# Cross-attention with float32 probabilities: score products in bursts of three pairs, softmax sums inverted as 128x16 by way of DRAM, last iteration's divide and split placed in the next stage's block

## The reference

```
q = (layernorm(x) @ Wq + bq)   k = (ctx @ Wk + bk)   v = (ctx @ Wv + bv)      # x 4096x512, ctx 3202x512
A = softmax(q k^T / sqrt(32))                     # per head, 4096 x 3202
x = x + (A v) @ Wo + bo
y = layernorm(x);  w = softmax(y @ WrT + br), all but the two largest set to 0
x = x + sum_e w[e] * (y @ We[e]^T + be[e])
```

## Time and profile before

| | |
|---|---|
| time, median of 3 runs | 2689.87 us (2685.3 to 2693.89) |
| the profiled execution, time | 2697.49 us |
| its span, first to last instruction | 2695.7 us |
| attention block, first score product to the next block's first load | 302.3 to 2212.3 us |
| TensorE busy over the span | 2560.7 us (95%) |
| VectorE busy | 2298.3 us (85%) |
| ScalarE busy | 1910.6 us (71%) |
| GpSimd busy | 383.2 us (14%) |
| mean granted TensorE clock | 0.97 of 2.4 GHz |

### The profile page before, as it was taken

One profiled execution on the slowest core, in us unless ns is written; L12 is line 12 of the kernel. 1 busy time (PEld: TensorE's weight loads), 2 busy tenths in 40 slices (PEclk: granted clock), 3 DMA queues, 4 the chain that ended last, 5 costly groups with the idle time before them and its releaser, 6 DMA issues. The chain is left out here.

```text
span 2695.7 us, 42991 instructions
## 1 busy us (share of the span) xinstructions
PE 2560.7 (95%) x14123; PEld 1286.6 (48%) x14123; DVE 2298.3 (85%) x1810; ACT 1910.6 (71%) x2141; POOL 383.2 (14%) x324
## 2 busy tenths in 40 slices
PE   8999399999999999999999999999999969879998
PEld 7878233333333333333333333333333327768776
DVE  4377399999999999999999999999999966657555
ACT  3123388888888888888888888888888845523333
POOL 2122100000000000000000000000000014315664
PEclk9999699999999999999999999999999989969999
DMA  7446841000051100005110000511000028724463
GB/s 254 160 153 213 189 120 39 22 21 20 21 118 24 37 20 21 21 21 118 25 36 21 20 21 20 118 28 33 21 21 21 21 67 310 250 83 132 126 216 125
DMA packets 125744, 222.77 MB, mean 83 GB/s; under 512 B 19666, under 2 KB 51930, under 8 KB 124772
## 3 DMA queue, kind: packets, MB, share of 16 engines
q1 hardware_dynamic: 110468, 177.57, 23.3%
q0 software_dynamic: 15072, 42.49, 5.0%
HBM read 146.67 MB, written 91.14 MB: 88 GB/s over the span
## 5 line engine op out<-in xcount | busy, mean ns | idle before, releaser
L964 ACT ACTIVATE probs<-psum 128x1024 f32<-128x1024 f32 x1664 | 1612.1, 1024 | 244.4 <-PE psum L1088 215.2
L1017 DVE TENSOR_TENSOR sums<-sums,probs 128x2048 f32<-128x2048 f32 x704 | 1647.3, 2340 | 44.8 <-ACT probs L964 19.4
L1088 PE MATMUL psum<-q_st,k_st 97*128 97x512 f32 x3328 | 1004.8, 423 | 49.5 <-DMA q_st<-shift_scratch 23.6
L1088 PEld LDWEIGHTS psum<-q_st,k_st 97*128 97x128 f32 x3328 | 563.0, 189 | 825.4 <-ACT probs L964 673.7
L1095 PE MATMUL psum<-probs,v_st 128*32 128x512 f32 x6656 | 890.1, 607 | 0.0
L821 POOL TENSOR_TENSOR o_low<-o_sb,o_high 128x512 fp32r<-128x512 f32 x32 | 74.4, 2325 | 1791.3 <-ACT o_high L938 1791.3
L1095 PEld LDWEIGHTS psum<-probs,v_st 128*32 128x32 f32 x6656 | 131.5, 108 | 308.2 <-ACT probs L964 219.1
L1764 PE MATMUL psum<-we_hi,wo 128*128 x624 | 219.7, 414 | 8.5 <-issue 5.8
L1617 ACT ACTIVATE wo<-psum 128x512 fp32r<-128x512 f32 x78 | 46.8, 600 | 138.3 <-PE psum L1750 101.8
L1764 PEld LDWEIGHTS psum<-we_hi,wo 128*128 128x128 f32 x624 | 120.4, 193 | 35.3 <-issue 9.6
L1674 DVE TENSOR_TENSOR res<-psum,be_all 128x512 f32<-128x512 f32 x78 | 53.9, 691 | 93.3 <-PE psum L1764 92.3
(11 more groups left out here) (184 smaller groups left out, 1890.6 us busy)
## 6 DMA issues: line engine op xcount, KB each, us to landing
q_st<-qh_scratch SPq DMA_DIRECT2D x64, 256.0 KB
token_rows<-rows SPq DMA_DIRECT2D x8, 1040.0 KB, 5.2
xn<-in_x SPq DMA_DIRECT2D x16, 512.0 KB, 6.6
qh_scratch<-o_hi SPq DMA_DIRECT2D x8, 1024.0 KB, 4.5
ql_scratch<-o_lo SPq DMA_DIRECT2D x8, 1024.0 KB, 7.7
q_st<-ql_scratch SPq DMA_DIRECT2D x32, 256.0 KB
token_rows<-in_x SPq DMA_DIRECT2D x1, 8192.0 KB, 30.4
oh_scratch<-o_high SPq DMA_DIRECT2D x128, 64.0 KB, 1.6
```

The costliest lines, as they stand in the source:

```text
L964: nc.scalar.activation(probs[:, p_slot[t], 2 * half:2 * half + 2, :], psum[:, 2 * slot:2 * slot + 2, :], ACT.Exp, scale=SCALE).then_inc(ex ...
L1017: nc.vector.tensor_tensor(sums[b][:], a[:], probs[:, p_slot[t]], ALU.add).then_inc(added, 1)
L1088: mm = nc.tensor.matmul(psum[:, 2 * slot + h % 2, :], k_st[:, h, t * P:(t + 1) * P], q_st[:, b, h, :], start=True, stop=True)
```

## The change

Five things:

- **Bursts.** TensorE's pairs are no longer issued two per tile: before a weigh, pairs are issued up to an index that closes a set of three slots. `weigh(t)` follows pair 2t+7 or up to two more (`LEAD` = 7), so bursts of three pairs alternate with one and with two weighs.
- **Sums inverted small.** ScalarE copies the sums out of PSUM before pair 14 (128x512). GpSimd writes their 4 distinct rows to DRAM and reads them back as 128x16. VectorE inverts those after its 10th add, GpSimd writes the inverses to DRAM and reads them back with four DMAs, each spreading one row over 32 partitions. VectorE multiplies after its 14th add (before: both after the 5th).
- **Split later.** ScalarE's `o_high` moves from before pair 24 to before pair 36.
- **Last iteration.** Its sum copy, inversion, product, split and stores move into `route_tokens`, among its first five steps.
- **Buffers.** `recip`, `o_sb`, `o_high`, `o_low` become one shared tensor, which `route_tokens` uses for `yn` and `mix_experts` for `xs` and one `res`; some semaphores are merged (`fold`, `chain`).

```diff
-DIVIDE_AT = 4
+SUMS_COPY_AT, INVERT_AT, NORMALISE_AT, SPLIT_AT = 14, 9, 13, 36
+LEAD = 7
...
+def spread_sums(pool, a, it):
+    pool.wait_ge(a["sums_copied"], it + 1)
+    pool.dma_start(a["sum_d"], a["recip"][0:P:DH, :]).then_inc(a["bounced"], 16)
+    pool.wait_ge(a["bounced"], it * 32 + 16)
+    pool.dma_start(a["spread"][:], a["sum_d"].rearrange("h (p f) -> (h p) f", p=DH)).then_inc(a["sums_spread"], 16)
+def broadcast_inverses(pool, a, it):
+    pool.wait_ge(a["inverted"], it + 1)
+    pool.dma_start(a["inv_d"].rearrange("h (p f) -> (h p) f", p=DH), a["spread_inv"][:]).then_inc(a["bounced"], 16)
+    pool.wait_ge(a["bounced"], it * 32 + 32)
+    for h in range(HG):
+        pool.dma_start(a["recip"][h * DH:(h + 1) * DH, :], a["inv_d"][h:h + 1, :].to_broadcast([DH, CH])).then_inc(a["inv_in"], 16)
+def invert_sums(dve, a, it):
+    dve.wait_ge(a["sums_spread"], it * 16 + 16)
+    dve.reciprocal(a["spread_inv"][:], a["spread"][:]).then_inc(a["inverted"], 1)
+def normalise(dve, a, it):
+    dve.wait_ge(a["inv_in"], it * (16 * HG) + 16 * HG)
+    dve.wait_ge(a["o_left"], it + 1)
+    dve.tensor_tensor(a["o_sb"], a["o_sb"], a["recip"], ALU.mult).then_inc(a["o_final"], 1)
...
-    SPLIT_AT = 24
...
-                group(NG - 1, True)
-                sp.wait_ge(o_stored, NIT * STORES)
+                sp.wait_ge(o_stored, (NIT - 1) * STORES)
...
+                def copy_sums(it):
+                    act.wait_ge(sums_ready, it + 1)
+                    if not (isinstance(it, int) and it == 0):
+                        act.wait_ge(o_final, it)
+                    act.activation(recip, psum[:, SUM_BANK, :], ACT.Copy).then_inc(sums_copied, 1)
...
-                def divide(it):
-                    dve.wait_ge(sums_ready, it + 1)
-                    nc.vector.reciprocal(recip[:], psum[:, SUM_BANK, :]).then_inc(inverted, 1)
...
+                def burst_end(u, t):
+                    e = 2 * t + LEAD
+                    return e + (S_RING - 1 - e - u) % S_RING
...
                     for t in range(NT):
-                        if t + LAG < NT:
-                            scores(it, u, i, t + LAG, first)
-                        elif i_next is not None:
-                            scores(it + 1, u + 1, i_next, t + LAG - NT)
+                        while n <= burst_end(u, t):
+                            if n < NP:
+                                scores(it, u, i, n, first)
+                            elif i_next is not None:
+                                scores(it + 1, u + 1, i_next, n - NP, False)
+                            n += 1
                         weigh(it, i, t)
...
+                    if i == STORE_STEP:
+                        sp.wait_ge(results["low_ready"], LAST + 1)
+                        store_result(sp, results, HEADS // HG - 1, 1, KT - 1)
...
+                if i == NORMALISE_STEP - 1:
+                    broadcast_inverses(pool, results, LAST)
...
+                    if i == NORM:
+                        act.wait_ge(results["low_ready"], LAST + 1)
+                        act.wait_ge(results["o_stored"], (LAST + 1) * STORES)
...
+                    if i == INVERT_STEP:
+                        invert_sums(dve, results, LAST)
+                    if i == NORMALISE_STEP:
+                        normalise(dve, results, LAST)
```

More of the change, by code:

```diff
@@ L693, in _, with last_results @@
                 sum_squares(NC - 1, Q_SUM_BANK, CH, q_squared, q_summed)
-                pe.wait_ge(folded, 1)
+                pe.wait_ge(fold, 3)
                 pe.transpose(psum[0:1, K_SUM_BANK, 0:P], norms[:], ident[:]).then_inc(norms_turned, 1)
+def last_results(sb, sem, dram, shared_rows, oh_d, ol_d, o_stored):
+    recip, o_sb = shared_rows[:, 0, :], shared_rows[:, 1, :]
+    o_high, o_low = (shared_rows[:, n, :].bitcast(F32R) for n in (2, 3))
+    spread = sb("spread", [P, CH // DH], F32)
+    spread_inv = sb("spread_inv", [P, CH // DH], F32)
+    sum_d, inv_d = (dram(name, [HG, CH], F32) for name in ("sum_scratch", "inv_scratch"))
+    sums_ready = sem("sums_ready")
+    sums_copied = sem("sums_copied")
+    bounced = sem("bounced")
+    sums_spread = sem("sums_spread")
+    inverted = sem("inverted")
+    inv_in = sem("inv_in")
+    o_left = sem("o_left")
+    o_final = sem("o_final")
+    high_ready = sem("o_high_ready")
+    low_ready = sem("o_low_ready")
+    return locals()
@@ new lines, in store_result @@
+def store_result(sp, a, j, b, k):
+    for part, dst in ((a["o_high"], a["oh_d"]), (a["o_low"], a["ol_d"])):
+        place = dst.rearrange("n (a d) k r -> n d a k r", d=DH)
+        for h in range(HG):
+            sp.dma_start(place[ds(j * HG + h, 1), :, 2 * b:2 * b + 2, ds(k, 1), :].rearrange("o d a x r -> (o d) a (x r)"),
+                         part[h * DH:(h + 1) * DH, :].bitcast(F32).rearrange("p (a r) -> p a r", a=2)).then_inc(a["o_stored"], 16)
+def spread_sums(pool, a, it):
[3 more added lines that the diff above has]
+    pool.dma_start(a["spread"][:], a["sum_d"].rearrange("h (p f) -> (h p) f", p=DH)).then_inc(a["sums_spread"], 16)
@@ L724, in attention @@
         wo_raw = sums[1]
-        recip = sb("recip", [P, CH], F32)
-        o_sb = sb("o_sb", [P, CH], F32)
-        o_high = sb("o_high", [P, CH], F32R)
-        o_low = sb("o_low", [P, CH], F32R)
+        recip, o_sb, o_high, o_low = (results[n] for n in "recip o_sb o_high o_low".split())
         mx = sb("mx", [P, TPC, HG, 2], F32)
@@ L820, in low, with divide @@
                         pool.wait_ge(o_stored, it * STORES)
-                    pool.tensor_tensor(o_low[:], o_sb[:], o_high[:].bitcast(F32), ALU.subtract).then_inc(low_ready, 1)
-                low(0)
-                with pool.Fori(1, NIT) as it:
+                    pool.tensor_tensor(o_low, o_sb, o_high.bitcast(F32), ALU.subtract).then_inc(low_ready, 1)
+                def divide(it):
+                    spread_sums(pool, results, it)
+                    broadcast_inverses(pool, results, it)
                     low(it)
+                for it in range(NIT - 1):
+                    divide(it)
             @block.sync
@@ L877, in result @@
                     sp.wait_ge(low_ready, it + 1)
-                    for part, dst in ((o_high, oh_d), (o_low, ol_d)):
-                        place = dst.rearrange("n (a d) k r -> n d a k r", d=DH)
-                        for h in range(HG):
-                            sp.dma_start(place[ds(j * HG + h, 1), :, 2 * b:2 * b + 2, ds(k, 1), :].rearrange("o d a x r -> (o d) a (x r)"),
-                                         part[h * DH:(h + 1) * DH, :].bitcast(F32).rearrange("p (a r) -> p a r", a=2)).then_inc(o_stored, 16)
+                    store_result(sp, results, j, b, k)
                 def step(j, c, b, k, reload, more=True):
@@ L944, in step @@
                             fetch(it - 1)
+                        if n == SUMS_COPY_AT and not first:
+                            copy_sums(it - 1)
                         if n == SPLIT_AT and not first:
@@ L1137, in step @@
                             sum_up(it - 1, (u + 1) % 2)
-                for t in range(LAG):
-                    scores(0, 0, 0, t, True)
                 step(0, 0, 0, 0)
```

114 lines of the change are left out of this document (64 added, 50 removed).

## The result

The changed kernel takes 2717.1 us (median of 4 runs, 2710.6 to 2717.3) against 2687.8 for the kernel before on the same chip. The ratio is 1.0092, 95% interval 1.0074 to 1.0110: 20 to 30 us slower, where 13 us less were forecast. The profiled execution took 2717.3 us, its span is 2715.5 us, 19.8 more than the span of 2695.7 before (the profiled execution of the kernel before was some 0.3% slower than its median, so the two spans differ by less than the ratio's 25 us).

A forecast was written before the change was run, and what follows sets the result against it. The prediction took TensorE and VectorE, each worth about 58 us per iteration, as the bounds. Bursts -8, later split +7 and last iteration -12 gave -13 us from the median 2689.9: 2677 us, range 2655 to 2712.

The forecast's parts named there:

- What bounds the kernel: Attention iteration: TensorE (57.85 us) and VectorE (58.3 us) both full; relieving one gains nothing beyond the other.
- Bursts, -8: TensorE in attention: the slot wait pays back most saved switches, leaving 57.6 us per iteration, -8 us over 31.
- 0.2 and 0.3 gained and 0.35 lost: Per iteration, us: 0.2 from the 6.34 us period, 0.3 from a product with ones, 0.35 lost to copy and split.
- the term of 0.3: About one of three products with ones per iteration falls into the short half and covers the slot wait: 0.3 us gained.
- jumps at nothing: Ends of the attention loops: the forecast had no term for them, with 57.85 us taken as the iteration before.
- Later split, +7: Group ends: keys queued behind the split land late, 2 to 4 us wait at each of three; +7 us (0 to 15).
- DRAM way, 0: Sums and inverses through DRAM: the way back takes 9.1 us of 10.2 free, hidden by 1.1 us only.
- The rival in which GpSimd and VectorE shut each other out: Way through DRAM is late because DMA issues and adds block each other: slower, about 2720 us; chance 0.2.
- Last iteration, -12: Attention's end: next block's loads start 17.4 us earlier, 5 us given back there; -12 us (-17 to -7).
- bursts pay in full: Rival: slot wait does not bind, TensorE needs 54.9 us and VectorE 55.1 per iteration; 2600 us; chance 0.08.
- a given 0.91 us: ScalarE starts its first exponential 0.91 us after the block of score products; used in the slot wait's chain.

The follow-up runs named there:

- bursts_alone_straight: The kernel before with bursts and ScalarE's loop as straight code, division, split and last iteration as before: ratio 0.9990 to the kernel before.
- half_before: The kernel before with half of the exponentials and adds left out from the second iteration on (output not the reference's): 2677.9 us.
- half_after: The changed kernel with half of the exponentials and adds left out from the second iteration on (output not the reference's): 2627.9 us in one run.
- waits_first: The changed kernel with one line moved, so ScalarE waits for the scores last, behind its slot's weigh and add: ratio 0.9975 to the kernel before.
- act_no_loop: The changed kernel with ScalarE's loop over 30 iterations written out as straight code: ratio 0.9876 to the kernel before.
- no_bursts: The changed kernel with its score pairs back in twos, one tile before each weigh: ratio 1.0076 to the kernel before.
- bursts_alone: The kernel before with only the score pairs in bursts of three: ratio 1.0013 to the kernel before.
- keys_ahead: The changed kernel with a group's next queries and first two pieces of keys and values issued ahead of the eight result stores: ratio 1.0044 to the kernel before.
- own_tail: The changed kernel with the last iteration's copy, inversion, multiplication, split and stores back in attention's own block: ratio 1.0121 to the kernel before.
- straight: The changed kernel with ScalarE's and TensorE's attention loops as straight code and next queries and first keys ahead of the result stores: 2629.4 us, ratio 0.9756.

## Why the prediction was wrong, step by step

**What bounds the kernel.** "Two engines are each worth about 58 us, and relieving one gains nothing beyond the other" held: bursts_alone_straight shows VectorE as the bound at 58.3 us per iteration, half_before TensorE's own 57.85.

**Bursts, -8.** The period of 6.34 us was right, and half_after confirms the 6.02 behind it. The quiet iterations give -4.5: the three ahead of the first jump take 173.1 us, so 57.7 each instead of the forecast 57.6 (and 175.0 less 173.1 is the 1.9 that a jump costs; waits_first loses as much to act_no_loop). Here the forecast had added wrongly: its own terms, 0.2 and 0.3 gained and 0.35 lost, give 0.15 per iteration and not 0.2 to 0.25, so -5 and not -8. How well the term of 0.3 fits by itself is not shown, because what the products with ones cover of the wait depends on their place in the bursts. Two of them should add 1.72 us; in the iteration at 488.6 they add 1.85 (8.19 us to the burst after next instead of 6.34), in the one at 611.1 they add 1.23 (13.91 for six tiles instead of 12.68). Of VectorE I had forecast 55.1 us of work and 2 us idle per iteration; the row above has 54.3 and 4.

**The step that failed: jumps at nothing.** The forecast took 57.85 as the iteration and let the ends of the loops stand. I had the 0.51 clock behind a pause in the earlier trace rows, and used it for the keys alone. Two things changed at a jump. ScalarE's pause grew from 1.3 to 2.3 us. Its part behind the branch grew from at most 3.0 to at least 3.3 us in every kernel with the copy of the sums in the loop, together with the third packet of instructions (no_bursts: 3.3 to 3.5 us, and a pause of 2.0 to 2.3; bursts_alone, with two packets: 2.7 to 2.9 us, and a pause of 1.4 to 1.7). And the bursts leave TensorE no slack, so that more of it passes. The longer pause costs 0.9 us each in the order of twos (no_bursts), and nothing more at TensorE's jumps. With the bursts it costs 9 x 1.4 (1.9 less 0.45), and 8 us at TensorE's four jumps, where the clock falls twice instead of once: +21 us that no term of my sum had. What the bursts do to the old, short pause is not shown: in bursts_alone VectorE's 58.3 us per iteration hide it. I had asked of each inserted instruction where it meets slack, and not what a loop's end does once that slack is used up.

**Later split, +7.** The mechanism and the wait were right (2.4, 3.1 and 4.4 us against 2 to 4). The size was off: each end adds 4.7 to 6.9 us, in all 15.5 more than before, just above the upper bound of 15. The waits on keys are 10.0 us of it. The rest follows them: the granted clock is at its lower level for 13.6 us in all (an estimate: half of that, 6.8 us, is lost), which the forecast had named as its upper end and not taken, and at the second group's end ScalarE's jump meets the loads. The bursts are no cause of it, since no_bursts has +19.7. keys_ahead takes back 12 in attention, 13 by the ratios.

**DRAM way, 0.** Right, with 3 us of margin instead of 1. The rival in which GpSimd and VectorE shut each other out is refuted at these issues: 0.50 us each, adds unchanged.

**Last iteration, -12.** Right: 17.0 earlier, 6.3 given back, -10.7 over the whole end, and 12.7 or 8 by own_tail.

Sum of what was measured: -4.5 + 21 + 15.5 - 10.7 - 1.3 (first iteration) - 0.4 (attention begins earlier) is +19.6; the span grew by 19.8. The rival "bursts pay in full" priced the missing slot wait at 54.9 us per iteration and 2600 in all. straight goes part of that way (56.6 per iteration), by a cause (ScalarE's wake-up) that stands in the forecast as a given 0.91 us.

**What stays open.** Why ScalarE's jump takes a third packet when its loop holds one instruction more was not tried: the loop's length and its place in memory move together. Why the clock falls twice at TensorE's jumps in the changed kernel and once in no_bursts, after pauses of like length (1.0 and 1.9 us in no_bursts at the second), is open too. Nor was it tried why the pause differs between kernels with the same loop (59.2 in the changed kernel, 61.2 us in own_tail for the same iteration).

## What to carry to other kernels

When a change makes one engine wait for another in every period, the way from semaphore to first instruction belongs to the period: put the wait that comes last in time also last in the code, with all computed counts ahead of it, or write the loop out. Before counting a saving in the steady state, price the loop ends and the reloads again with the slack that is left after the change. And of a step that is moved, follow the queue behind it: what needs no result of the step goes ahead of it.
